# A graph and slot-mixing layer on one core: a node's loop edge is weighted in from its own row instead of gathered

## The reference

```python
src = jnp.concatenate([_s, _d, loop])          # 50000 random edges, both directions, then one loop edge a node
dst = jnp.concatenate([_d, _s, loop])
order = jnp.argsort(dst, stable=True)          # so each node's run of edges ends with its own loop edge
src, dst = src[order], dst[order]

def gcn_conv(x, edge_index, W, b, n_nodes):
    loop = jnp.arange(n_nodes)
    src = jnp.concatenate([edge_index[0], loop])   # and a second loop edge a node
    dst = jnp.concatenate([edge_index[1], loop])
    deg = segment_sum(ones, dst)
    dinv = rsqrt(deg)
    h = x @ W.T
    return segment_sum(h[src] * (dinv[src] * dinv[dst])[:, None], dst) + b

x = x + gcn_conv(relu(gcn_conv(layernorm(x), ...)), ...)
x = x + slot_block(layernorm(x))
```

## Time and profile before

| | |
|---|---|
| Median of 3 runs | 3055.51 us (3054.37 to 3058.86) |
| The profiled execution | 3031.99 us, of which the span of its instructions is 3030.3 us |
| Instructions in the span | 27648 |
| Moved by DMA | 876.71 MB, mean 289 GB/s |
| Of it by POOL's gathers (queue q0) | 671.74 MB |

### The profile page before, as it was taken

The page is one execution under the profiler, slowest core; times in us unless marked ns, Lnnn a source line. Parts: engine busy times, 40 slices in busy tenths (PEclk is TensorE's granted clock), DMA queues, the critical chain, the costliest instruction groups (busy, mean ns, idle before and its releaser), DMA issues.

```text
span 3030.3 us, 27648 instructions
## 1 busy us (share of the span) xinstructions
PE 2157.9 (71%) x7718; PEld 1314.9 (43%) x7719; DVE 1812.2 (60%) x2352; ACT 531.4 (18%) x985; POOL 1838.2 (61%) x1853
## 2 busy tenths in 40 slices
PE   6616777767677767777656777777777777777768
PEld 6613444434344434444323444444444444444424
DVE  7646566666666656666546566666656666666416
ACT  7830101111101010111001111111111111111300
POOL 3247676666666767666566666666666666666100
PEclk9997888888888888888877888888988888888889
DMA  9488888888888888888678988888888888888648
GB/s 332 175 338 301 287 291 293 291 285 288 287 291 293 300 292 290 295 289 292 229 261 296 315 312 303 301 302 298 307 299 305 314 305 307 295 301 316 237 148 311
DMA packets 237825, 876.71 MB, mean 289 GB/s; under 512 B 63260, under 2 KB 64044, under 8 KB 237756
## 3 DMA queue, kind: packets, MB, share of 16 engines
q0 software_dynamic: 143808, 671.74, 64.3%
q1 hardware_dynamic: 66132, 162.17, 14.8%
q10 hardware_dynamic: 27836, 42.21, 3.8%
HBM read 826.10 MB, written 82.00 MB: 300 GB/s over the span
## 4 chain that ended last, share of the span: by engine, by line
issue 23%; DVE 21%; another core or an unknown queue 19%; DMA 13%; POOL 12%; PE 6%; ACT 3%; DVEq 1%; POOLq 0%; ACTq 0%; SPq 0%
DVE acc L1116 14%; POOL rows L662 11%; DMA rows<-table_layer,gidx 10%; PE work L1360 2%; ACT logits L727 1%; DVE work L1135 1%; ACT xsT L716 1%; DVE hot L1075 1%; DVE agg L1116 1%; PE left L1386 1%; DMA rows<-xnew 1%; DMA out_x<-xstage 1%; PE acc L1485 1%; PE left L1436 0%
## 5 line engine op out<-in xcount | busy, mean ns | idle before, releaser
L662 POOL DMA_INDIRECT rows<-table_layer,gidx x1764 | 1760.1, 998 | 795.6 <-issue 484.2
L1116 DVE TENSOR_TENSOR acc<-acc,rows 128x768 f32<-128x768 f32 x1176 | 1134.0, 964 | 403.6 <-DMA rows<-table_layer,gidx 199.8
L1360 PE MATMUL work<-WT,aggT 128*128 128x384 f32 x2352 | 893.4, 542 | 262.0 <-DVE row_idx L1025 175.0
L1386 PE MATMUL left<-rows,hot 128*128 128x384 f32 x1960 | 812.9, 550 | 186.9 <-issue 97.6
L1360 PEld LDWEIGHTS work<-WT,aggT 128*128 128x128 f32 x2352 | 504.2, 217 | 660.4 <-issue 219.9
L1386 PEld LDWEIGHTS left<-rows,hot 128*128 128x128 f32 x1960 | 383.9, 211 | 468.6 <-issue 188.7
L816 ACT ACTIVATE aggT<-fixed 128x768 f32<-128x768 f32 x98 | 79.4, 810 | 1642.2 <-remote 1554.5
L1347 PE MATMUL fixed<-ident,xs 128*128 128x128 f32 x294 | 70.8, 409 | 228.2 <-issue 208.1
L1006 DVE TENSOR_TENSOR pick_col<-slot_of,work 128x6 f32<-128x6 f32 x49 | 7.9, 161 | 280.0 <-remote 273.5
L1347 PEld LDWEIGHTS fixed<-ident,xs 128*128 128x128 f32 x294 | 53.4, 212 | 262.0 <-issue 239.0
L786 ACT ACTIVATE acc<-rows 128x768 f32<-128x768 f32 x98 | 79.8, 814 | 434.3 <-issue 312.6
(11 more groups left out here) (309 smaller groups left out, 1330.2 us busy)
## 6 DMA issues: line engine op xcount, KB each, us to landing
self_row<-table_layer SPq DMA_DIRECT2D x98, 384.0 KB
rows<-table_layer,gidx POOLq DMA_INDIRECT x1764
xstage<-in_x SPq DMA_DIRECT2D x67, 384.0 KB
xs<-in_x SPq DMA_DIRECT2D x58, 384.0 KB
xnew<-xs SPq DMA_DIRECT2D x49, 384.0 KB
table_layer<-ynext SPq DMA_DIRECT2D x48, 384.0 KB
table_layer<-xstage ACTq DMA_DIRECT2D x40, 384.0 KB
xstage<-xnew SPq DMA_DIRECT2D x21, 384.0 KB, 5.7
```

The costliest lines, as they stand in the source:

```text
L662: pool.indirect_dma_start(rows[:, slot, :], None, table[l][0:ROWS, :], bass.IndirectOffsetOnAxis(ap=gidx[:, k % 2, slot:slot + 1], axis=0) ...
L1116: dve.tensor_tensor(acc[:, :, 0:H] if n < OWN - 1 else halves(agg[:, :]), acc[:, :, 0:H], halves(row), ALU.add).then_inc(S["added"], 1)
L1360: m = pe.matmul(work[:, h, 0:H], aggT[:, kc, :], WT[l][:, kc, h * H:(h + 1) * H], start=kc == 0, stop=kc == KC - 1)
L1386: m = pe.matmul(left[:, h, 0:H], hot[:, b, c, :], rows[:, slot, h * H:(h + 1) * H], start=c == 0, stop=c == LEFT - 1)
```

## The change

The loop edge at the end of a node's run is no longer gathered. `OWN` goes from 13 to 12, so a step has 12 own and 5 left gathers, and the lists are built for `deg - 1` edges. DVE's last addition of a step becomes `self_row * self_weight + acc` with a weight of two per node (one, where the tile takes the general path). The threshold from which edges are "left" stays where it was, at 13 edges with the loop edge (`LISTED`). `rows` keeps its 18 slots in size (`RING`); the last one is unused in the layers.

That a run ends with a loop edge is checked on the chip: for each edge whose successor has another target, source and target must be equal. A fault is counted with the faults of order, and any fault selects the general path for all tiles. For this SP loads `src` as well, and instead of the shifted copy of `dst` only its first column, one element for each of 124 partitions. The check stands at group 2 of the one-hot groups instead of behind the last.

```diff
-OWN = 13
+OWN = 12
 LEFT = 5
 CHUNKS = OWN + LEFT
+RING = CHUNKS + 1
+LISTED = OWN + 1
-RUNS = ((0,), (1, 2, 3), (4, 5), (6, 7, 8), (9, 10), (11, 12))
+RUNS = ((0,), (1, 2, 3), (4, 5), (6, 7), (8, 9), (10, 11))
...
+            sp.dma_start(src_flat, a["src"].rearrange("(p c) -> p c", p=EP)).then_inc(s["runs_in"], 16)
             sp.wait_ge(s["cleared"], 1)
-            sp.dma_start(dn_flat[0:EP - 1, :],
-                         a["dst"][1:1 + (EP - 1) * EC].rearrange("(p c) -> p c", p=EP - 1)).then_inc(s["misc_in"], 16)
-            sp.dma_start(dn_flat[EP - 1:EP, 0:EC - 1],
-                         a["dst"][1 + (EP - 1) * EC:E].rearrange("(p c) -> p c", p=1)).then_inc(s["misc_in"], 16)
+            sp.dma_start(d_after[0:EP - 1, :], a["dst"].rearrange("(p c) -> p c", p=EP)[1:EP, 0:1],
+                         allow_slow_non_contiguous=True).then_inc(s["runs_in"], 16)
...
+            def check_runs():
+                dve.wait_ge(s["runs_in"], 32)
+                one.mark(dve.tensor_tensor(viol, d_next, d_flat, ALU.is_lt))
+                one.mark(dve.tensor_tensor(run_end, d_next, d_flat, ALU.not_equal))
+                one.then(dve.tensor_tensor(not_own, src_flat, d_flat, ALU.not_equal))
+                one.then(dve.tensor_tensor(run_end, run_end, not_own, ALU.mult))
+                one.then(dve.tensor_tensor(viol, viol, run_end, ALU.add))
+                one.then(dve.tensor_reduce(vsum, viol, AX.X, ALU.add))
+
             for g in range(GROUPS):
+                if g == 2:
+                    check_runs()
...
-            one.then(dve.tensor_tensor(viol, dn_flat, d_flat, ALU.is_lt))
-            one.then(dve.tensor_reduce(vsum, viol, AX.X, ALU.add))
...
-                one.then(dve.tensor_tensor(eff_deg, deg[:, 0:T], usable_bc, ALU.mult))
+                one.mark(dve.scalar_tensor_tensor(self_weight[:, :], deg[:, 0:T], 1.0, usable_bc, ALU.min, ALU.mult))
+                one.then(dve.scalar_tensor_tensor(eff_deg, deg[:, 0:T], 1.0, usable_bc, ALU.subtract, ALU.mult))
+                one.mark(dve.tensor_scalar(self_weight[:, :], self_weight[:, :], 1.0, None, ALU.add))
...
-                        dve.tensor_tensor(acc[:, :, 0:H] if n < OWN - 1 else halves(agg[:, :]), acc[:, :, 0:H],
-                                          halves(row), ALU.add).then_inc(S["added"], 1)
+                        if n < OWN - 1:
+                            dve.tensor_tensor(acc[:, :, 0:H], acc[:, :, 0:H], halves(row), ALU.add).then_inc(S["added"], 1)
+                        else:
+                            dve.scalar_tensor_tensor(halves(agg[:, :]), halves(row), self_weight[:, ds(t, 1)],
+                                                     acc[:, :, 0:H], ALU.mult, ALU.add).then_inc(S["added"], 1)
```

More of the change, by code:

```diff
@@ L110, in build @@
         logits = sb("logits", [P, T, SLOTS])
-        rows = sb("rows", [P, CHUNKS, D])
+        rows = sb("rows", [P, RING, D])
         hot = sb("hot", [P, 2, PICKS, P])
@@ L117, in build @@
         left_end = sb("left_end", [P, T])
+        self_weight = sb("self_weight", [P, T])
         below = sb("below", [P, P])
@@ L256, in chunk @@
             def chunk(t, i):
-                first = sp.value_load(over_first[0:1, ds(t, 1)], min_val=0, max_val=E + WINDOW)
+                first = sp.value_load(over_first[0:1, ds(t, 1)], min_val=0, max_val=E + WINDOW + P)
                 sp.wait_ge(O["chunk_added"], nth)
@@ L351, in x_buf @@
             return xbuf[(n if n < RELOADED else n - PARKED) % XBUFS]
-        d_flat, dn_flat, d_high_i, d_low_i = (flat[0:EP, c * EC:(c + 1) * EC].bitcast(i32) for c in range(4))
-        viol = flat[0:EP, 2 * EC:3 * EC]
-        halfs = flat[:, 4 * EC:].bitcast(bf16)
+        wide_ec = EC + 2
+        d_flat, src_flat, d_high_i, d_low_i = (flat[0:EP, c * wide_ec:c * wide_ec + EC].bitcast(i32) for c in range(4))
+        d_next, d_after = flat[0:EP, 1:EC + 1].bitcast(i32), flat[0:EP, EC:EC + 1].bitcast(i32)
+        viol, run_end = (flat[0:EP, c * wide_ec:c * wide_ec + EC] for c in (2, 3))
+        not_own = flat[0:EP, wide_ec:wide_ec + EC]
+        halfs = flat[:, 4 * wide_ec:].bitcast(bf16)
         d_high, d_low = halfs[0:EP, 0:EC], halfs[0:EP, EC:2 * EC]
@@ L593, in _ @@
         def _(pool):
-            pool.memset(dn_flat[:, EC - 1:EC], N).then_inc(s["cleared"], 1)
+            pool.memset(d_after, N).then_inc(s["cleared"], 1)
             for ap, steps in ((iota_low, [[1, P], [0, GROUP]]), (iota_high, [[1, T], [0, GROUP]]),
@@ L904, in _ @@
                                   ).then_inc(s["onehots_ready"], 1)
-            dve.wait_ge(s["misc_in"], 96)
-            one.then(dve.tensor_tensor(viol, dn_flat, d_flat, ALU.is_lt))
-            one.then(dve.tensor_reduce(vsum, viol, AX.X, ALU.add))
+            dve.wait_ge(s["misc_in"], 64)
             dve.wait_ge(s["onehots_used"], GROUPS)
             one.then(dve.tensor_copy(deg[:, 0:T], mm[:, 0, 0:T]))
-            one.mark(dve.tensor_scalar(degs[:, 1, 0:T], deg[:, 0:T], float(OWN), 0.0, ALU.subtract, ALU.max))
-            one.then(dve.tensor_scalar(degs[:, 2, 0:T], deg[:, 0:T], float(OWN + EXTRA), 0.0, ALU.subtract, ALU.max))
+            one.mark(dve.tensor_scalar(degs[:, 1, 0:T], deg[:, 0:T], float(LISTED), 0.0, ALU.subtract, ALU.max))
+            one.then(dve.tensor_scalar(degs[:, 2, 0:T], deg[:, 0:T], float(LISTED + EXTRA), 0.0, ALU.subtract, ALU.max))
             dve.wait_ge(one.sem, one.n)
@@ L957, in _ @@
             one.then(dve.tensor_scalar(ends, ends, float(E), None, ALU.add))
-            one.then(dve.tensor_scalar(past, usable, float(WINDOW), None, ALU.mult))
+            one.then(dve.tensor_scalar(past, usable, float(WINDOW + P), None, ALU.mult))
             one.then(dve.tensor_tensor(past, tot, past, ALU.add))
```

2 lines of the change are left out of this document (1 added, 1 removed).

## The result

| | kernel before | changed kernel |
|---|---|---|
| Median (fastest to slowest) | 3054.94 us (3050.82 to 3058.86), 4 runs | 2930.65 us (2921.23 to 2935.55), 4 runs |
| Ratio | | 0.9594, 95% interval 0.9571 to 0.9617 |
| Profiled execution, span | 3031.99, 3030.3 us | 2926.26, 2924.6 us |

The change takes 124.3 us off, by the interval 117 to 131. The forecast was -127 us and 2928.

The account below looks back on a forecast made before the run. POOL's stream of gathers at 1.306 us each plus one stop a step was taken as the bound. -128.0 us for gathers and +1.0 for setup gave -127 us: 2905 profiled, 2928.5 by the median, range 2898 to 2972.

Parts of the forecast that it names:

- POOL, -128.0 us: In the layers' steps, 98 gathers fewer at 1.306 us each, all on the path: -128.0 us.
- DVE at 0: In the layers, 98 additions fewer and a third operand in the last one, both costed at 0; 90 us if path.
- The stop constant: POOL's one wait in each layer step, 2.7 us, stays as long; 0.3 us either way would be 29 us.
- The reason for the stop: PE's signals come late while POOL streams gathers and get through some 2 to 4 us after POOL stops.
- the pattern of this kernel: In setup and layers, PE's signals are late while POOL streams, and come some 2 to 4 us after it stops.
- the stop goes: Rival: the shorter stream lets PE's signals through, up to 265 us more go, 2664 us; chance 0.04, wholly or in part.
- Transfers bound: Rival: a layer step costs its DMA transfers, one less saves 125 us in all, 2931 us; chance 0.10.
- A second stop: Rival: POOL stops again before left 3, 3.15 us a step; 3236 us, or 3082 in layer 2 alone; chance 0.03.
- Setup +1.0 us: Before the layers: +0.4 small operations, -0.3 narrower window shifts, +0.9 load of single elements; check hidden; ends -0.3 and +8.
- the load of single elements: In setup, SP's load of 124 single elements delays later loads by 0 to 4.3 us; 0.9 us taken, at most about 1.3.

Follow-up runs that it names:

- e1_gather_back: Changed kernel with an 18th gather put back in each step, which DVE waits for but does not add; 2749.32 us, ratio 1.0003 to the kernel before.
- e2_add_back: Changed kernel, still 17 gathers a step, with DVE adding one row more in each step; 2619.91 us, ratio 0.9529 to the kernel before.
- a1_changed: Changed kernel unaltered, on a chip where the kernel before took 3033.93 us; 2898.17 us, ratio 0.9563 to the kernel before.
- e6_pause: Changed kernel with four waited-for fills of a spare tile holding POOL's gathers about 2.2 us in each step; 2875.79 us, ratio 0.9483 to the kernel before.
- e4_half_rows: Changed kernel with its twelve own gathers moving half a row each, still 17 gathers a step; 2617.69 us, ratio 0.9522 to the kernel before, two repeats.

## Why the prediction was right

**POOL, -128.0 us: right; shown where there is no stop, argued where there is one.** The gathers went at 1.306 us each. Without a stop the gain was 128.3 us, gone again with the gather (e1_gather_back) and untouched by DVE's additions (e2_add_back). On the chips with a stop, where the forecast was made and measured, neither of the two was run. There only the size speaks for the gather: the intervals of the two measurements, 117 to 131 and 124 to 141 us, hold the 128.0 and shut out both nothing and the 90 us that DVE's additions alone would have been worth.

**DVE at 0: right where there is no stop.** There e1_gather_back took the additions away and left the gathers as they were, and the time stayed within -2 and +3 us. With a stop it wasn't tested. The new operation took 1014 ns, as the nearest row had it.

**The stop constant: right within what can be told.** By the profiled executions a step became 1.07 us shorter, not 1.31: 105.7 us between the two spans, as if the stop had grown by 0.24 us. But that execution of before lay 23.5 us under its median, which is 0.24 us a step, and the medians differ by 124.3 here and by 136 in a1_changed. The forecast's -127 lies in both intervals. So the stop's length differs from one execution to the next by as much as the traces differ, and neither a growth nor a shrinking by the change is shown. The forecast had taken +-0.3 us a step for it.

**The reason for the stop: it fits here, and not in general.** The prediction took it for "the pattern of this kernel" that PE's signals come late while POOL streams. The trace after shows it as foretold, with three engines going on at once, 2.7 us after POOL's end. (The prediction's own 2.3 us is 2.4 by its rows: from 2290.52 to 2292.96.) That e6_pause has almost no stop left agrees with it. On the other chips the same program had neither lag nor stop: 0.04 us for the transposes. What was wrong is "while POOL streams": after a stop or a pause the signals are prompt again for some gathers (L808, and L834 in e6_pause). The rival "the stop goes" had 2664 us for it; 2619 and 2748 are what the changed kernel's relatives and the kernel before take where there is none. It isn't the length of the stream that decides, since the kernel before has its 18 gathers in a row on both kinds. It goes with the chip, as far as so few chips can tell (one chip was met twice, without a stop both times); that the forecast met a chip of the same kind as its own trace is luck that it didn't count on.

**Transfers bound: refuted on the chips without the stop** (e4_half_rows, three times), and open on the others. It would have given 2931, which this result can't tell from the forecast; the reason, not the number, needed the experiment. The Trainium skill, "SBUF — State Buffer", section "A bandwidth-pool intuition that's wrong (but worth ruling out)", takes HBM for the bottleneck almost always. On the chips without a stop the rule had more for it than the prediction could know: its estimate from that page was 22.0 us for a step of layer 2 with one transfer less, and e2_add_back's step took 22.1 us, at 345 GB/s. The same time a step in layer 1, with one transfer less, speaks against it, and e4_half_rows settles it: 31% fewer bytes changed no time, so the measurement decides against the rule for this kernel.

**A second stop: did not come,** with 96 waits for 98 steps. But its margin was not the 4.7 us that the prediction read. In the step shown PE's last sum before the release, left 3, is stretched over POOL's stream and ends at 2205.73, 0.8 us after the release (2204.93) and 0.1 us after POOL went on. The condition named for the rival was met, and yet no second stop followed; the point from which it decides was wrong. A signal that just misses the release isn't held through the next stream, since signals are prompt for some gathers behind a stop (L808 above).

**Setup +1.0 us: +1.5, by other terms.** The first gather of the layers stands at 224.4 instead of 222.9 (in a1_changed at 223.3, so a microsecond of it can be the execution's own). The timeline of the changed kernel has the load of 124 single elements (L453), the old load of tiny pieces (L462), what starts ACT (L721), the constant that PE waits for (L628) and the check (L902 to L907):

```profile
1.64 0.33 SPq L453 DMA_DIRECT2D rows<-in_dst  x1
...
5.37 3.33 SPq L462 DMA_DIRECT2D small<-in_scale  x1
...
14.37 1.28 ACT L721 ACT_TABLE_LOAD   x1 [14.37 <-DMA dst_pad<-pad_edges]
...
18.67 1.13 DVE L902 TENSOR_TENSOR rows<-rows 125x850 f32<-125x850 int32 x1
...
20.96 1.08 POOL L628 TENSOR_SCALAR_AFFINE_SELECT steps_down<-ident 128x128 f32<-128x128 f32 x1
...
22.10 3.26 PE L1298 MATMUL left<-rows 125*128 125x49 bf16 x34 [22.10 <-POOL steps_down L628]
...
24.09 1.04 DVE L907 TENSOR_REDUCE small<-rows 125x1 f32<-125x850 f32 x1
25.47 2.43 DVE L916 TENSOR_TENSOR rows<-rows 125x4352 bf16<-125x4352 bf16 x1 [0.34 <-PE left L1298]
...
119.30 0.21 DVE L923 COPY hid<-left 128x49 f32<-128x49 f32 x1 [4.59 <-PE left L1298]
...
126.58 0.49 ACT L739 ACTIVATE small<-small 128x50 f32<-128x50 f32 x3 [3.71 <-DVEq L962]
```

The check runs from 18.67 to 25.13 (forecast 18.95 to 25.4), and the next group starts at 25.47 (25.4), so DVE's part is hidden as said. What was not seen is that POOL is slower beside it. PE's first product waits for a constant that POOL builds, and in the kernel before POOL had it at 19.93:

```profile
19.65 0.28 POOL L623 TENSOR_SCALAR_AFFINE_SELECT steps_down<-ident 128x128 f32<-128x128 f32 x1
```

Its last three constants of 128 x 128 took 0.28, 0.29 and 0.28 us while DVE was idle, and 0.98, 1.09 and 1.08 us beside the check, in the changed kernel's trace and in those of a1_changed, e1_gather_back and e2_add_back alike. So PE starts at 22.10 instead of 19.99, and it is later through all groups: 0.8 us at their end (119.30 against 118.53) and 1.0 us at ACT's roots (126.58 against 125.60). That the check is the reason was not tested by a run without it.

The 0.9 us that the forecast took for the load of single elements did not come. That load is L453, and SP is through with it in 0.33 us, where the forecast had let itself be guided by the 4.55 us of another load. ACT starts at 14.37 instead of 16.06, earlier and not later. Nor did the upper bound of 1.3 us follow from the rows given for it: 4.3 less 3.47 us is 0.8. That +1.5 stands close to +1.0 is luck: one term was missing and one too many.

**What stays open.** What in the chip holds PE's signals back, why some chips have it, whether it is the gathers' traffic or their issue, and how short a pause is enough. Open is also what the gather and DVE's additions are worth one by one where there is a stop, and whether fewer than 17 gathers pay as much there.

## What to carry to other kernels

Take the pace of a loop as so many instructions of the streaming engine times their interval, plus the stop, and look for what ends the stop: if several engines go on together, long after the work they wait for has ended, their own work is not what to shorten. Whatever shortens the stream then pays in full until another engine becomes the limit (here between 17 and 14 gathers), and removing work from the other engines pays little or nothing. Before a gain is credited to a term smaller than the spread of the executions, compare how far the profiled execution lies from its own median, and measure on more than one chip. A piece of work that is hidden in an engine's idle time may still slow the engine beside it.

## What the runs showed of the hardware

- The same program took 3034 to 3055 us on some chips and 2748 to 2749 us on others. 2.7 us a step, 265 us in 98 steps, would be most of the 286 to 306 us between them.
- Where there is a stop, PE's signals lag 8.9 us in a long stream of gathers and 0.04 us soon after a pause. DVE's 49 operations that wait for PE's search (L1022 in the changed kernel, from 170.7 us in setup to 1396.9 at the end of layer 1) show the lag too: 48 waits end by "remote" and sum to 283.2 us; in e1_gather_back only two waits are left, 4.0 us in sum.
- POOL's gathers of 128 rows start every 1.30 to 1.31 us whether a row has 3072 or 1536 bytes (e2_add_back 591, e4_half_rows 590 in 770 us).
- The same three POOL instructions took 0.28 to 0.29 us with DVE idle and 0.98 to 1.09 us beside DVE's check.
- Where there is a stop, a pause put in on purpose made the kernel 22 us faster (e6_pause against a1_changed).
